# Two kinds of transfer of the rotary attention layers issued by ScalarE instead of SP

## The chip, the core and the metric

The kernel runs on one core of a Trainium2 chip. The metric is the device time of one execution in microseconds, lower is better. In this text TensorE (PE in the profile) does the matrix products, VectorE (DVE) and ScalarE (ACT) work element by element, GpSimd (POOL) adds and fills, and SP is the engine that issues transfers. Each engine takes its own instructions in the order in which they stand; engines wait for each other by semaphores.

## What is computed

```python
x = x + _layernorm(_L0_attn_ref(_layernorm(x), ...))   # one attention block, 16 heads of 8, and an MLP
x = x + _layernorm(_L0_ffn_ref(_layernorm(x), ...))    # L = 4 layers, below

for l in range(L):                       # x is (2, 1024, 128)
    h = _rms(x, ln1_w[l])
    q, k, v = h @ wq, h @ wk, h @ wv     # 16 query heads, 4 key heads, head size 64
    q = q * c + _rot_half(q) * sn        # _rot_half: concatenate([-x[..., 32:], x[..., :32]])
    k = k * c + _rot_half(k) * sn
    attn = softmax(q k^T / 8 + causal_bias)
    x = clip(x + (attn @ v) @ wo, -100, 100)
    x = clip(x + _moe(_rms(x, ln2_w[l]), ...), -100, 100)   # 8 experts, the best 2 weighted
```

All in float32; the kernel splits float32 operands into a high and a low half where precision needs it.

## The kernel before

The first block and its MLP take about the first 600 us. Then come the four layers, each about 675 us: some 500 us in which attention runs, and some 175 us in which the experts run and the next layer's first head is prepared beside them.

Attention is tiled by head group. `n` (0 to 7, `HEADS`) is a pair of a batch row and one of the 4 key heads with its 4 query heads. The 1024 positions of a group are two chunks `c` of 512 columns. For each group and chunk a preparation runs, and its steps have letters that the code uses as names:

- `P`: TensorE projects two query pairs and the key (`u` = 0, 1, 2, three products each), VectorE multiplies each result by the sine table into `rb` and by the cosine table into `ra` (lines 2099 and 2100).
- `R`: four DMAs copy `rb` to `rbp` with the halves of 32 rows swapped (line 1118). They need all three `P` of the chunk, told by the semaphore `s_rp`.
- `A`: GpSimd adds `rbp` to `ra` (line 1240); `H`, `L`, `K`: ScalarE, GpSimd and VectorE split the result into high and low halves; `Q`: five DMAs (lines 1127 and 1131) put them into the stacks `qs`, `ks`.
- `M`: TensorE forms scores of a query tile against keys (line 1756) and VectorE takes row maxima (line 2112). `J`: TensorE turns the maxima (line 1766), ScalarE copies them negated to `mrow` (line 1423), and one DMA writes them into a row of `qs` (line 1138), so that the later product of scores has the maximum subtracted.

Group `n` itself is attended at the same time as group `n + 1` is prepared. A step has a query tile `t` (0 to 7) and a key tile `kt` up to `t`: `S` on TensorE (lines 1784, 1785, and 1787 on the diagonal) into one of two banks, the exponential on ScalarE (line 1416) into one of four `prob` tiles, the running sum on GpSimd (line 1223), `V` on TensorE (line 1801). At the end of a tile come `D` (TensorE line 1816, then VectorE lines 2086 and 2088, the normalised result `att`) and `O` (TensorE line 1823, VectorE line 2207). `S` of a step needs the exponential of the step two before; the exponential needs `V` and the sum of the step four before.

What the engines do in which order isn't written by hand. `network_order()` lists every step with a cost in ns and what it needs (`stage(engine, name, cost, *after)`), and `planned` fills each engine's list greedily by these costs. So a changed cost or engine of one stage moves others. `("sync", ...)` is SP, `("land", ...)` the time until a transfer has landed. Before, `R` stood on SP at 2500 ns and the DMA of `J` on SP at 560 ns, beside all other transfers:

```python
stage("sync", ("R", l, n, c), 2500, ("vector", ("P", l, n, c, u)), ...)
stage("scalar", ("J", l, n, c), 280, ("tensor", ("J", l, n, c)), ...)
stage("sync", ("J", l, n, c), 560, ("scalar", ("J", l, n, c)))
```

In layer 0 the end of the first MLP still runs beside the first group: `Row Nm` (ScalarE line 1292, eight instructions) scales the last rows, after which GpSimd fills stacks with constants (`Zero 1`, lines 1231 to 1234) before it takes up sums and `A` again.

Of the kernel before, what the change touches and what calls it, by code (L numbers as in the profile page):

```python
# [7 lines left out]
F32 = mybir.dt.float32  # L8
# [6 lines left out]
P = 128  # L15
B, SEQ, D = 2, 1024, 128
TPB = SEQ // P
# [8 lines left out]
L, NH, NKV, HD, FF, E = 4, 16, 4, 64, 256, 8  # L26
# [7 lines left out]
NCH = SEQ // CH  # L34
TPC = TPB // NCH
HEADS = NKV * B
# [132 lines left out]
PASSES = NG1 * B  # L169
# [222 lines left out]
def network_order():  # L392
# [72 lines left out]
    def ring_item(l, item):  # L465
# [9 lines left out]
        if what == "P":  # L475
            c, u = part
# [15 lines left out]
            stage("sync", ("R", l, n, c), 2500, ("vector", ("P", l, n, c, u)), older and ("gpsimd", ("A", *older, 2)), *routed)  # L492
            stage("land", ("R", l, n, c), 3400, ("sync", ("R", l, n, c)))
# [3 lines left out]
        elif what == "M":  # L497
            t, m = part
            _, w, k0, k1 = max_pieces(t)[m]
            stage("tensor", ("M", l, n, t, m), w * max(115, (k1 - k0) / 2.2) + (90 + w * 35) * (k1 == (t + 1) * P), ("land", ("Q", l, n, t // TPC)),  # L500
                  ("vector", ("K", l, n, t // TPC)), *turn)
            stage("vector", ("M", l, n, t, m), 150 + 1.04 * w * (k1 - k0), ("tensor", ("M", l, n, t, m)),
                  ("tensor", ("J", l, n - 1, t // TPC)) if n else None)
        else:
            c = part[0]
            if c:
                stage("vector", ("X", l, n), 180, last["vector", "M"])
            stage("tensor", ("J", l, n, c), 200, ("vector", ("X", l, n)) if c else last["vector", "M"], *turn)
            stage("scalar", ("J", l, n, c), 280, ("tensor", ("J", l, n, c)), ("land", ("J", l, n - 1, c)) if n else None)
            stage("sync", ("J", l, n, c), 560, ("scalar", ("J", l, n, c)))  # L510
            stage("land", ("J", l, n, c), 1800, ("sync", ("J", l, n, c)))
# [126 lines left out]
    for b in range(B):  # L638
# [4 lines left out]
             "W", "K", "H", "R", "Q", "J", "A", "X", "L", "D", "O", "V", "S", "P", "M", "Zk", "Za", "Zb", "Zs", "Zv", "Zd", "Zi", "Zr", "Zo"]  # L643
# [10 lines left out]
def program(nc, x_in, ln1_g, ln1_b, Wq, Wk, Wv, Whq, Whk, Wo, ln2_g, ln2_b, W1, b1, W2, b2,  # L654
            f_ln1, f_ln2, wq, wk, wv, wo, wr, wg, wu, wd, cos_in, sin_in, out):
    with ExitStack() as ctx:
# [273 lines left out]
        def _(sp):  # L930
# [115 lines left out]
            for what, *i in NETWORK["sync"]:  # L1046
# [59 lines left out]
                else:  # L1106
                    l, n, c, *part = i
                    b, u = n % 2, (l * HEADS + n) * NCH + c
                    if what == "R":
                        if l and n == 0 and c == 0:  # L1110
                            sp.wait_ge(s_rv, N_ROUTE * B * l)
                            sp.wait_ge(s_gd, 16 * B * l)
                        if u == 0:
                            sp.wait_ge(s_pv1, PASSES * 2 * TPB)
                        sp.wait_ge(s_rp, 6 * u + 6)
                        for k in range(4):
                            to, of = k * 32, (k ^ 1) * 32
                            sp.dma_start(rbp[to:to + 32, :, :], rb[of:of + 32, :, :]).then_inc(s_rot, 16)
                    elif what == "Q" and part[0] == 0:
# [12 lines left out]
                    elif what == "J":  # L1132
                        sp.wait_ge(s_mc, u + 1)
                        if l == 0 and n < 2:
                            sp.wait_ge(s_zero, 3 * n + 3)
                        if l and n == 1:
                            sp.wait_ge(s_qz, NCH * (l - 1) + c + 1)
                        sp.dma_start(qs2[b][0:1, c, :, :].bitcast(F32).rearrange("a h (t n) -> a (h t) n", t=TPC),
                                     mrow2[c][:, :].bitcast(F32)).then_inc(s_rw[c], 16)
# [121 lines left out]
        def _(a):  # L1261
# [100 lines left out]
            for what, *i in NETWORK["scalar"]:  # L1362
# [61 lines left out]
                elif what == "H":  # L1424
# [15 lines left out]
                    else:  # L1440
                        act(ks[b][0:HD, 0, cs], ra[0:HD, 2, :], ACT.Copy).then_inc(s_hi, 1)
                        act(ks[b][HD:P, 1, cs], ra[HD:P, 2, :], ACT.Copy).then_inc(s_hi, 1)
                elif what == "Ge":
# [872 lines left out]
```

## Time and profile before

| what | value |
|---|---|
| median of 3 runs | 3379.39 us (3378.13 to 3379.53) |
| the profiled execution | 3370.07 us, span of its instructions 3368.3 us |
| TensorE busy | 3164.6 us, 94% of the span |
| VectorE, GpSimd, ScalarE busy | 76%, 60%, 51% |
| mean granted clock of TensorE | 0.98 of full speed |

The profiled execution is one execution; its own time is 9.3 us under the median of the runs, and 1.8 us of it lie around the span. Each row of a timeline gives a start in us, a length, the engine and line, what is written and read, the number of merged instructions, and in brackets the time that the engine sat idle before and what ended that. Of the SP queue a row is an issue, that is the time in which the issuing engine is held by it, and not the transfer. A TensorE row ends by a model, so its starts are the better measure. The digits of 40 slices give each engine's busy share in tenths.

### The profile page before, as it was taken

Reading aid. Unit: us, or ns where it says so; the run is one execution under the profiler, and the core shown is the slowest. Engines: PE = TensorE matmul, PEld = TensorE weight load, DVE = VectorE, ACT = ScalarE, POOL = GpSimd, SP = SyncE. Lnnn points to the kernel's source line nnn. Section 1 sums busy time; section 2 is a strip of 40 time slices with the busy share of each in tenths; the row PEclk is TensorE's granted clock in tenths of the full one; section 3 lists DMA queues with packets and bytes.
Section 4 is the critical chain, followed back from the end, with each engine's and each line's share of the span. In section 5 each row is a group of like instructions: output and inputs, shape, how many; then the busy total and the mean of one; then the engine's idle time right before and its main releaser. Section 6 shows DMA issues by size and latency. Waiting matters only on the chain.

```text
span 3368.3 us, 51429 instructions
## 1 busy us (share of the span) xinstructions
PE 3164.6 (94%) x17792; PEld 2094.8 (62%) x17792; DVE 2567.0 (76%) x3764; ACT 1705.9 (51%) x3083; POOL 2010.1 (60%) x1573
## 2 busy tenths in 40 slices
PE   5899998799999999999999999999999999999998
PEld 3455554566666677666666776666667766666576
DVE  7778775777887678778886788778867788788667
ACT  4566667444434474444344755443446553443465
POOL 2100000288868665778777657787776577877765
PEclk8899999899999999999999999999999999999999
DMA  5342421332222154332231543232215532232153
GB/s 121 72 72 51 90 47 37 83 85 67 68 66 69 41 171 136 86 73 64 67 71 31 183 139 86 61 76 67 61 34 187 138 90 60 67 76 60 27 176 114
DMA packets 160402, 283.61 MB, mean 84 GB/s; under 512 B 32592, under 2 KB 64208, under 8 KB 159888
## 3 DMA queue, kind: packets, MB, share of 16 engines
q1 hardware_dynamic: 160144, 280.31, 33.1%
q8 instruction: 145, 2.38, 0.3%
q14 instruction: 113, 0.93, 0.1%
HBM read 88.47 MB, written 31.72 MB: 36 GB/s over the span
## 4 chain that ended last, share of the span: by engine, by line
PE 52%; DVE 6%; ACT 3%; issue 2%; POOL 1%; DMA 1%; SPq 0%; DVEq 0%; ACTq 0%
PE psA L1801 11%; PE psA L1784 7%; PE psA L1756 6%; PE psA L1785 5%; PE psA L1828 3%; PE psA L1829 3%; PE psA L1830 3%; PE psA L1816 3%; DVE rden L2086 2%; PE psA L1823 2%; DVE mxp L2112 2%; PE psA L1865 1%; PE psA L1759 1%; PE psA L1866 1%; PE psA L1867 1%
## 5 line engine op out<-in xcount | busy, mean ns | idle before, releaser
L1416 ACT ACTIVATE prob<-psA 128x512 f32<-128x512 f32 x1152 | 652.7, 595 | 1045.9 <-PE psA L1785 462.3
L1223 POOL TENSOR_TENSOR xw<-xw,prob 128x512 f32<-128x512 f32 x672 | 868.1, 1292 | 230.8 <-ACT prob L1416 157.1
L2112 DVE TENSOR_REDUCE mxp<-psA 128x1 f32<-128x512 f32 (+3 forms) x864 | 528.9, 665 | 57.4 <-PE psA L1756 35.0
L2086 DVE RECIPROCAL rden<-psA 128x256 f32<-128x256 f32 x256 | 449.1, 1754 | 131.3 <-PE psA L1816 128.6
L1784 PE MATMUL psA<-qs,ks 128*128 128x512 f32 x1152 | 523.8, 455 | 21.1 <-ACT prob L1416 19.8
L1756 PE MATMUL psA<-ks,qs 128*128 128x512 f32 (+3 forms) x1536 | 475.4, 385 | 11.3 <-DMA qs<-qs 5.4
L1257 POOL TENSOR_TENSOR hidl<-gate,hidh 128x512 fp32r<-128x512 f32 x256 | 331.3, 1302 | 210.9 <-ACT hidh L1471 209.0
L1785 PE MATMUL psA<-qs,ks 128*128 128x512 f32 x1152 | 453.8, 394 | 0.0
L1223 POOL TENSOR_TENSOR xw<-prob 128x512 f32<-128x512 f32 x224 | 288.1, 1286 | 271.4 <-issue 127.2
L2034 DVE TENSOR_REDUCE mxp<-psA 128x1 f32<-128x1024 f32 x256 | 304.5, 1220 | 84.8 <-PE psA L1591 83.7
L1335 ACT ACTIVATE pr<-psA 128x512 f32<-128x512 f32 x512 | 274.6, 600 | 122.0 <-PE psA L1610 115.8
L1756 PEld LDWEIGHTS psA<-ks,qs 128*128 128x128 f32 x1536 | 269.8, 193 | 84.1 <-issue 32.0
L1784 PEld LDWEIGHTS psA<-qs,ks 128*128 128x128 f32 x1152 | 220.3, 191 | 142.7 <-issue 68.5
L1801 PE MATMUL psA<-prob,vv 128*64 128x256 f32 x2304 | 292.2, 387 | 6.4 <-DVE inner L2207 3.7
L1801 PE MATMUL psA<-prob,outer 128*64 128x256 f32 x2304 | 293.5, 386 | 5.0 <-DVE inner L2207 5.0
L2112 DVE TENSOR_REDUCE mxq<-psA 128x1 f32<-128x384 f32 (+3 forms) x352 | 209.7, 637 | 107.7 <-PE psA L1759 105.6
L1240 POOL TENSOR_TENSOR rab<-rab,rbp 128x512 f32<-128x512 f32 x192 | 247.0, 1301 | 34.9 <-DMA rbp<-rab 34.9
L2238 DVE TENSOR_TENSOR gate<-psA,spread 128x512 f32<-128x512 f32 x256 | 176.1, 688 | 100.5 <-ACT psA L1465 99.0
L1169 POOL TENSOR_TENSOR feat<-feat,smr 128x1024 f32<-128x1024 f32 x16 | 30.6, 1914 | 364.5 <-DVE smr L2017 364.5
L1785 PEld LDWEIGHTS psA<-qs,ks 128*128 128x128 f32 x1152 | 218.4, 190 | 21.5
L1828 PE MATMUL psA<-xh,eh 128*128 128x512 f32 x512 | 210.9, 412 | 17.6 <-DVE gate L2238 10.4
L1801 PEld LDWEIGHTS psA<-prob,vv 128*64 128x64 f32 x2304 | 154.8, 137 | 103.8 <-issue 25.2
(222 smaller groups left out, 5833.0 us busy)
## 6 DMA issues: line engine op xcount, KB each, us to landing
qs<-normed SPq DMA_DIRECT2D x256, 256.0 KB, 4.3
rbp<-rab SPq DMA_DIRECT2D x256, 192.0 KB, 3.5
spread<-routing_weights SPq DMA_DIRECT2D x128, 256.0 KB, 3.6
qs<-qs SPq DMA_DIRECT2D x64, 256.0 KB, 3.2
expert_weight_halves<-eh SPq DMA_DIRECT2D x32, 384.0 KB, 2.4
expert_weight_halves<-el SPq DMA_DIRECT2D x32, 384.0 KB, 3.8
eh<-expert_weight_halves SPq DMA_DIRECT2D x32, 384.0 KB, 3.2
el<-expert_weight_halves SPq DMA_DIRECT2D x32, 384.0 KB, 3.9
```

The lines of the kernel that those rows point to most:

```text
L1223: g.tensor_tensor(psum_k[:, t % 2, :], before, prob[:, i % 4, :], ALU.add).then_inc(s_su, 1 if kt > 1 else 2 + (t == 1))
L1257: g.tensor_tensor(hidl[:, n % 3, :], gate[:, n % GATES, :], hidh[:, n % 3, :], ALU.subtract).then_inc(s_hl, 1)
L1335: act(pr1[:, j % 2, h, :], psS1[:, n % 3, :], ACT.Exp).then_inc(s_ex1, 1)
L1416: act(prob[:, k % 4, :], psS[:, k % 2, :], ACT.Exp, scale=float(HD) ** -0.5).then_inc(s_ex, 1)
L1756: ins = mm(bank[:, i, :], qs1[b][:, c, h + i, t % TPC * P:(t % TPC + 1) * P], ks[b][:, 0, k0:k1], start=(i == 0), stop=not diagonal)
L1784: mm(psS[:, i % 2, :], ks[b][:, 0, tile], qs1[b][:, c, :, qs], start=True, stop=False)
L1785: ins = mm(psS[:, i % 2, :], ks[b][:, 1, tile], qs2[b][:, c, :, qs], start=False, stop=(kt < t))
L1801: ins = mm(psO[t % 2][q * HD:(q + 1) * HD, 0:256], vv[b][:, kt, g * HD:(g + 1) * HD], prob[:, i % 4, q * 256:(q + 1) * 256], start=(kt == ...
L1828: mm(dst, eh[held(w)][:, w0:w0 + P], xh[:, cs], start=True, stop=False)
L2034: vec.tensor_reduce(mxp1[:, p % 2, c, h * 4 + t:h * 4 + t + 1], pair("M", p, c, t, h), AX.X, ALU.max).then_inc(s_mx1, 1)
L2086: vec.reciprocal(rden[:, :], psO[t % 2][:, 256:512]).then_inc(s_rd, 1)
L2112: vec.tensor_reduce(dst, bank, AX.X, ALU.max).then_inc(s_mr, 1)
```

## The change

`R` and the DMA of `J` are issued by ScalarE's own queue. The waits that stood before them on SP go with them to ScalarE. For the planner `R` is a stage of ScalarE of 1200 ns, the DMA of `J` a new stage `Jr` of ScalarE of 300 ns that follows the copy. The transfers themselves, their sizes and the buffers are the same. All else stays on SP.

```diff
-            stage("sync", ("R", l, n, c), 2500, ("vector", ("P", l, n, c, u)), older and ("gpsimd", ("A", *older, 2)), *routed)
-            stage("land", ("R", l, n, c), 3400, ("sync", ("R", l, n, c)))
+            stage("scalar", ("R", l, n, c), 1200, ("vector", ("P", l, n, c, u)), older and ("gpsimd", ("A", *older, 2)), *routed)
+            stage("land", ("R", l, n, c), 3400, ("scalar", ("R", l, n, c)))
...
-            stage("sync", ("J", l, n, c), 560, ("scalar", ("J", l, n, c)))
-            stage("land", ("J", l, n, c), 1800, ("sync", ("J", l, n, c)))
+            stage("scalar", ("Jr", l, n, c), 300, ("scalar", ("J", l, n, c)), ("gpsimd", ("Zero", n)) if l == 0 and n < 2 else None)
+            stage("land", ("J", l, n, c), 2200, ("scalar", ("Jr", l, n, c)))
...
+                elif what == "R":
+                    l, n, c = i
+                    u = (l * HEADS + n) * NCH + c
+                    if l and n == 0 and c == 0:
+                        a.wait_ge(s_rv, N_ROUTE * B * l)
+                        a.wait_ge(s_gd, 16 * B * l)
+                    if u == 0:
+                        a.wait_ge(s_pv1, PASSES * 2 * TPB)
+                    a.wait_ge(s_rp, 6 * u + 6)
+                    for k in range(4):
+                        to, of = k * 32, (k ^ 1) * 32
+                        nc.scalar.dma_start(rbp[to:to + 32, :, :], rb[of:of + 32, :, :]).then_inc(s_rot, 16)
+                elif what == "Jr":
+                    l, n, c = i
+                    u = (l * HEADS + n) * NCH + c
+                    a.wait_ge(s_mc, u + 1)
...
+                    nc.scalar.dma_start(qs2[n % 2][0:1, c, :, :].bitcast(F32).rearrange("a h (t n) -> a (h t) n", t=TPC),
+                                        mrow2[c][:, :].bitcast(F32)).then_inc(s_rw[c], 16)
```

The branches `R` and `J` of SP's list are gone. What ScalarE does in a row, in layer 1 while group 3 is attended and group 4 prepared (`prob<-psA` is an exponential, `mrow` the copy of `J`, `normed<-rab` a step `H`). Before:

```order
617 L1416 ACTIVATE prob<-psA 128x512 x5
618 L1423 ACTIVATE mrow_1<-psA 16x128
619 L1416 ACTIVATE prob<-psA 128x512 x9
620 L1439 ACTIVATE normed<-rab 128x512
621 L1416 ACTIVATE prob<-psA 128x512 x2
```

And now:

```order
675 L1398 ACTIVATE prob<-psA 128x512 x7
676 L1405 ACTIVATE mrow_1<-psA 16x128
677 L1445 DMA qs_1<-mrow_1 1x16x128
678 L1398 ACTIVATE prob<-psA 128x512 x3
679 L1436 DMA rbp<-rab 32x1536 x4
680 L1398 ACTIVATE prob<-psA 128x512 x4
681 L1421 ACTIVATE normed<-rab 128x512
```

The four swaps of chunk 1 stand between the exponentials of the tiles `t = 4`, `kt = 1` and `kt = 2`. TensorE at the same place, the scores of `kt = 2` to `kt = 4` of that tile (lines 1784, 1785) and the product `O` of tile 3 (`wos,att`). Before:

```order
3590 L1784 MATMUL psA<-qs_1,ks 128x512
3591 L1785 MATMUL psA<-qs_1,ks 128x512
3592 L1756 MATMUL psA<-ks,qs_0 128x384
3593 L1759 MATMUL psA<-maskq,identb 128x128
3594 L1784 MATMUL psA<-qs_1,ks 128x512
3595 L1785 MATMUL psA<-qs_1,ks 128x512
3596 L1787 MATMUL psA<-maskk,identb 128x512
3597 L1784 MATMUL psA<-qs_1,ks 128x512
3598 L1785 MATMUL psA<-qs_1,ks 128x512
3599 L1823 MATMUL psA<-wos,att 128x128 x2
```

And now:

```order
3570 L1788 MATMUL psA<-qs_1,ks 128x512
3571 L1789 MATMUL psA<-qs_1,ks 128x512
3572 L1760 MATMUL psA<-ks,qs_0 128x384
3573 L1763 MATMUL psA<-maskq,identb 128x128
3574 L1827 MATMUL psA<-wos,att 128x128 x2
3575 L1788 MATMUL psA<-qs_1,ks 128x512
3576 L1789 MATMUL psA<-qs_1,ks 128x512
3577 L1791 MATMUL psA<-maskk,identb 128x512
```

`O` of tile 3 has moved ahead of two products of scores. ScalarE at the start of layer 0, where group 1 is prepared; `inner<-qT,rstd` is `Row Nm`. Before:

```order
219 L1285 ACT_TABLE_LOAD
220 L1285 ACTIVATE std<-vsum,eps 128x8
221 L1292 ACTIVATE inner<-qT,rstd 128x128 x8
222 L1423 ACTIVATE mrow_1<-psA 16x128
223 L1377 ACTIVATE normed<-inner 128x512 x2
```

And now:

```order
223 L1267 ACT_TABLE_LOAD
224 L1267 ACTIVATE std<-vsum,eps 128x8
225 L1405 ACTIVATE mrow_1<-psA 16x128
226 L1445 DMA qs_0<-mrow_1 1x16x128
227 L1436 DMA rbp<-rab 32x1536 x4
228 L1274 ACTIVATE inner<-qT,rstd 128x128 x8
```

`Row Nm` now stands behind the copy of maxima and behind five issues.

## Rows read from the trace of the kernel before

**Rows 1.** The page: busy us of each engine, share of the span, instructions.

```profile
PE 3164.6 (94%) x17792; PEld 2094.8 (62%) x17792; DVE 2567.0 (76%) x3764; ACT 1705.9 (51%) x3083; POOL 2010.1 (60%) x1573
```

**Rows 2.** TensorE: who it waited for; us in total, times, longest us.

```profile
PE psA L1823 <- DVE att L2088: 31.2, 35, 1.1
...
PE psA L1784 <- ACT prob L1416: 19.8, 43, 2.3
...
PE psA L1756 <- DMA qs<-qs: 5.4, 3, 2.4
```

**Rows 3.** SP's queue: what it waited for, same columns.

```profile
SPq L1138 <- ACT mrow L1423: 519.9, 60, 36.4
SPq L1118 <- DVE rab L2100: 335.1, 59, 10.0
```

**Rows 4.** SP's issues by line: count, ns min/median/max, first and last start.

```profile
L1118 SPq DMA_DIRECT2D rbp<-rab x256: 507/591/1786, 606.0 to 3110.2; - x128
...
L1138 SPq DMA_DIRECT2D qs<-mrow x64: 526/563/575, 639.9 to 3164.6; - x64
...
L1127 SPq DMA_DIRECT2D qs<-normed x256: 598/660/2005, 614.7 to 3122.8; - x128
...
L1105 SPq DMA_DIRECT2D spread<-routing_weights x128: 319/327/1253, 1145.9 to 3334.6; - x128
```

**Rows 5.** Windows: length; busy us (count) of PE, PEld, DVE, ACT, POOL; clock; DMA.

```profile
600.00:700.00 100.00, 82.76 (x392) 53.86 (x392) 71.97 (x120) 46.63 (x89) 43.44 (x34) 0.86 0.37 94
...
1498.90:1562.15 63.25, 61.64 (x379) 40.57 (x379) 50.41 (x78) 25.41 (x46) 48.36 (x39) 1.00 0.29 68
```

**Rows 6.** Timeline, ScalarE: start, us, line, tiles, count, idle time before.

```profile
1556.49 0.60 ACT L1416 ACTIVATE prob<-psA 128x512 f32<-128x512 f32 x1 [0.88 <-PE psA L1787]
1560.44 1.09 ACT L1416 ACTIVATE prob<-psA 128x512 f32<-128x512 f32 x2 [3.35 <-PE psA L1785]
1562.18 1.08 ACT L1416 ACTIVATE prob<-psA 128x512 f32<-128x512 f32 x2 [0.65 <-PE psA L1785]
```

**Rows 7.** Timeline, SP's queue: start, us, line, count.

```profile
1560.63 2.46 SPq L1118 DMA_DIRECT2D rbp<-rab  x4
```

**Rows 8.** Timeline, VectorE.

```profile
1559.92 0.68 DVE L2100 TENSOR_TENSOR rab<-psA,cosT 128x512 f32<-128x512 f32 x1
...
1562.30 0.42 DVE L2088 TENSOR_TENSOR att<-psA,rden 128x256 f32<-128x256 f32 x1
```

**Rows 9.** Timeline, TensorE.

```profile
1562.83 0.50 PE L1784 MATMUL psA<-qs,ks 128*128 128x512 f32 x1
...
1564.09 0.61 PE L1823 MATMUL psA<-wos,att 128*128 128x128 f32 x4
1564.45 0.42 PE L1756 MATMUL psA<-ks,qs 128*128 128x384 f32 x1
```

**Rows 10.** Timeline, TensorE, three waits around a group.

```profile
1547.05 0.71 PE L1823 MATMUL psA<-wos,att 128*128 128x128 f32 x4 [0.96 <-DVE att L2088]
...
1548.53 0.83 PE L1801 MATMUL psA<-prob,outer 128*64 128x256 f32 x5 [0.31 <-DVE inner L2207]
...
1586.52 0.50 PE L1784 MATMUL psA<-qs,ks 128*128 128x512 f32 x1 [0.29 <-ACT prob L1416]
```

**Rows 11.** Timeline, VectorE, between two chunks.

```profile
1589.26 5.47 DVE L2112 TENSOR_REDUCE mxp<-psA 128x1 f32<-128x512 f32 x9 [1.03 <-PE psA L1756]
```

**Rows 12.** Timeline, ScalarE and GpSimd, start of layer 0.

```profile
667.88 2.44 ACT L1292 ACTIVATE inner<-qT,rstd 128x128 f32<-128x128 f32 x8 [4.72 <-DVE rstd L1979]
670.26 0.27 ACT L1423 ACTIVATE mrow<-psA 16x128 fp32r<-16x128 f32 x1
...
670.38 3.50 POOL L1231 MEMSET qs<- 64x4096 f32 x1 [21.75 <-ACT inner L1292]
...
675.91 1.26 POOL L1223 TENSOR_TENSOR xw<-prob 128x512 f32<-128x512 f32 x1
```

**Rows 13.** Timeline, GpSimd, a change from experts to attention.

```profile
1272.68 3.80 POOL L1240 TENSOR_TENSOR rab<-rab,rbp 128x512 f32<-128x512 f32 x3 [1.81 <-DMA rbp<-rab]
```

More of the change, by code:

```diff
@@ L642, in network_order @@
              "Ew", "Eh", "El", "Es", "Er", "Hf", "Hw", "Hh", "Hl", "Si", "Y", "Ug", "Uu", "Aw", "Wa", "Wb",
-             "W", "K", "H", "R", "Q", "J", "A", "X", "L", "D", "O", "V", "S", "P", "M", "Zk", "Za", "Zb", "Zs", "Zv", "Zd", "Zi", "Zr", "Zo"]
+             "W", "K", "H", "R", "Q", "J", "Jr", "A", "X", "L", "D", "O", "V", "S", "P", "M", "Zk", "Za", "Zb", "Zs", "Zv", "Zd", "Zi", "Zr", "Zo"]
     return planned(plan, kinds, 150, 150, "VD", 110, {"vector": 120})
@@ L1108, in _ @@
                     b, u = n % 2, (l * HEADS + n) * NCH + c
[L1109 to L1119, printed above, removed]
+                    if what == "Q" and part[0] == 0:
                         if l and n == 1:
@@ L1131, in _ @@
                         sp.dma_start(qs2[b][HD:P, c, 0:GQ:2, :].bitcast(F32), qs2[b][0:HD, c, 1:GQ:2, :].bitcast(F32)).then_inc(s_dup, 16)
[L1132 to L1139, printed above, removed]
             sp.wait_ge(s_out, 16 * NCH * B)
@@ L1442, in _ @@
                         act(ks[b][HD:P, 1, cs], ra[HD:P, 2, :], ACT.Copy).then_inc(s_hi, 1)
+                elif what == "R":
[14 more added lines that the diff above has]
+                    a.wait_ge(s_mc, u + 1)
+                    if l == 0 and n < 2:
+                        a.wait_ge(s_zero, 3 * n + 3)
+                    if l and n == 1:
+                        a.wait_ge(s_qz, NCH * (l - 1) + c + 1)
+                    nc.scalar.dma_start(qs2[n % 2][0:1, c, :, :].bitcast(F32).rearrange("a h (t n) -> a (h t) n", t=TPC),
+                                        mrow2[c][:, :].bitcast(F32)).then_inc(s_rw[c], 16)
                 elif what == "Ge":
```

## The prediction

> **What bounds the kernel now.** I read the page first. TensorE is busy for 3164.6 us of 3368.3, the other engines for 76% or less [rows 1], so there are about 204 us in all in which TensorE is not at work, and nothing that merely relieves SP can give back more. Then the windows. While a group is attended the pattern repeats exactly every 63.25 us, with TensorE busy for 61.6 of it at full clock and ScalarE for 25.4 [rows 5]. The first 100 us of the layers are looser: TensorE 82.8 of 100 [rows 5]. Then who waits. TensorE's waits for transfers of the layers come to 5.4 us in three places, and its longest named waits in the layers are 31.2 us for `att` of VectorE and 19.8 us for exponentials [rows 2]. SP waits 519.9 us at the row of maxima and 335.1 us at the swap [rows 3]: it stands there before its data exist, it isn't late with them. In the group shown the swaps are issued at 1560.63 [rows 7], 0.03 us after the multiplication that they need has ended, at 1559.92 + 0.68 = 1560.60 [rows 8]. So the queue that the change relieves delays nearly nothing, and the engine that it loads sits in a loop (scores, exponential, values) with TensorE.
>
> **What moves.** 256 swaps of 0.591 us and 64 rows of 0.563 us [rows 4] are 151 + 36 = 187 us of issuing that leave SP and go to ScalarE. ScalarE's busy time doesn't show an issue, but the engine can't start an exponential during it. Per chunk that is four issues, 2.46 us [rows 7], and one of 0.56 us. No row shows an issue from ScalarE. The nearest are SP's own of the same transfers, 0.59 us each. From below the shortest plain issue bounds it, 0.327 us, from above that of the other transfers between buffers on the chip, 0.660 us at the median, 0.83 us in a row of four (3.32 us) [rows 4]. I take SP's 0.59.
>
> Perfetto Trace Analysis in the Trainium skill (section DMA Instruction, HWDGE) says that the recorded window of an issue is the time in which the issuing sequencer is held, lock and descriptors included, and Advanced Engine Details and Errata (Clock Domains) gives SP's and ScalarE's sequencers the same clock. By these the 0.59 us would hold on ScalarE as well, and the sum would be mine; the rows of before show issues on SP alone.
>
> **The row of maxima (`Jr`).** It follows the copy on ScalarE, which was the releaser on SP as well. In the loop ScalarE sat idle 0.88 us after the copy of chunk 1 before the next exponential, which waited for TensorE [rows 6]; 0.56 us fits in. In chunk 0 the planner's new order puts the copy ahead of an exponential that waits for `V` anyway. I cost `Jr` at nothing; without that cover it would be 64 x 0.56 = 36 us at most.
>
> **The swap of chunk 1.** By the new order it stands between the exponentials of `kt = 1` and `kt = 2` of tile 4. The first two exponentials start at 1560.44 and, 0.49 us later, at 1560.93, and end at 1561.53; that of `kt = 2` starts at 1562.18 [rows 6]. The sine products are ready at 1560.60. The issues can begin when the second exponential has started, 1560.93, or at the latest when it has ended, 1561.53. They end at 1563.39 or 1563.99, and the exponential is ready 0.60 us after that: 1563.99 or 1564.59. TensorE needs it for the scores of `kt = 4`, at 1562.83 before [rows 9]. Now `O` of tile 3 stands ahead of these, 1564.45 - 1564.09 = 0.36 us [rows 9], with its `att` ready at 1562.72 [rows 8]; TensorE gets to the scores at 1563.19. The stall is 0.80 to 1.40 us. I take 0.85, near the lower end, since two exponentials in a row take 1.09 us and not 1.20 [rows 6]: ScalarE takes its next instruction while the last runs. There are 24 such places (groups 2 to 7 of 4 layers): + 20.4 us (19 to 34).
>
> **The swap of chunk 0.** It stands behind the exponential of `kt = 1` of tile 7. Between the scores whose exponential it delays and those that need that exponential, the new order has another product of scores, five maxima pieces, a block of values and a `D`, over 2.5 us of TensorE's work by TensorE's pace [rows 9], 0.2 to 0.5 us each,. The cost is between nothing and chunk 1's 0.85 us; I take nothing. Without the cover it would be 20 x 0.85 = 17 us.
>
> **The new order.** Around a group TensorE waits three times, 0.96 + 0.31 + 0.29 = 1.56 us [rows 10]. The first two come from VectorE, late with `D` and `O` because it ran through its maxima late: it sat idle for 1.03 us before their first [rows 11], while TensorE did three blocks of values. The new list puts the first maxima pieces directly behind the scores, moves `O` and `D` of VectorE, and puts the fifth block of values ahead of the sixth scores, so that the 0.29 us go. Against that the `D` that TensorE waits for has one maxima piece more ahead of it, about 0.6 us (5.47 us for 9) [rows 11]. Bounds are 0 and 1.56 us per group. I take a third, 0.5 us, in 20 places (groups 3 to 7): - 10 us (0 to - 31).
>
> **Layer 0.** Here the window had TensorE idle for 17 us [rows 5]. Before, `Row Nm` ran from 667.88 to 670.32, and only then could GpSimd fill the stacks, 670.38 to 675.8, before it took up sums at 675.91 [rows 12] and worked on without a pause. Now the copy of maxima (not before 670.26), its issue and the four swaps come first: 670.26 + 0.27 + 0.56 + 2.46 = 673.6, and `Row Nm` ends 2.44 us later, at 676.0. GpSimd starts 5.7 us late. Sums and `A` queue behind it, and TensorE's `D` and ScalarE's exponentials behind these. TensorE idles there, so a part is covered: + 4 us (0 to 5.7).
>
> **The three changes from experts to attention.** The swap of the next layer's first chunk stands between steps of expert units. GpSimd's two next steps are then about 2.5 us later and end some 1.1 us after the 1272.68 at which it took up the rotation, having idled 1.81 us before it [rows 13]. The rotation's transfers then end TensorE's wait of up to 2.4 us for `qs` [rows 2]. With 0.4 us for the second chunk, 1.5 us each: + 4.5 us (0 to 10).
>
> **The sum.** 20.4 - 10 + 4 + 4.5 = + 18.9 us. Against the profiled execution's own 3370.07 us that is 3389.0. The median of the runs is 9.3 us above that execution; I carry this difference over unchanged: 3379.4 + 18.9 = 3398 us. A change under 0.2%, 6.8 us, I count as none: a measurement of this kernel can't tell it.
>
> DMA: Bandwidth & Descriptors in the Trainium skill (section Issuing engines are not separate DMA queues) says that issuing from several engines saves the issuing sequencer's time alone, as the transfers run on the same DMA engines. The trace agrees as far as it goes: what is saved is time of a queue that waits 519.9 and 335.1 us for its data [rows 3]. By that rule alone the time would stay 3379; the rule counts no loss where the other queue belongs to an engine with work.
>
> **Rivals.**
> 1. Faster: VectorE catches up wholly. Its 1.03 us go and with them all 1.56 us of TensorE's waits per group, - 31 us. This decides once more than 1.45 us per group come back, since the rest costs 28.9; with 0.59 us per issue it ends at 3377. With an issue of 0.45 us the stall of chunk 1 is 0.85 - 0.55 = 0.3 us, 7 us in all, the rest about 6, and the time 3362. For it: VectorE's idle time is real, and TensorE's work per group is the same. Against it: the extra maxima piece.
> 2. Issues on ScalarE at 0.33 us: 1.3 us for four, ending at 1562.2, no stall. Then - 10 + 2.5 + 2.5 = - 5: 3374. For it nothing in the trace but that plain issues are that short [rows 4]; the swaps never were under 0.507.
> 3. Issues at 0.83 us: 3.32 us for four, a stall of 1.71 us in 24 places, 41 us, with 5 and 6 for the rest and 10 back: 3421. This would also come from both queues contending for one generator of descriptors; in the attention of a group SP has nothing to issue at these moments, which speaks against it.
> 4. The stall is there but is covered: the 0.85 us come back at the later waits of the same group, as these wait for VectorE and not for TensorE. Then 8.5 + 3 us at most are left less 10: 3381. Against it: between the stall and the next wait VectorE waits for TensorE, so a shift of TensorE shifts both.
>
> **Chances.** The forecast with its own range, 3386 to 3410, has 0.47, of which 0.02 lie within 0.2%. Rival 1 has 0.14, half of it under 3372.6; rival 2 0.15, a third of it under that; rival 3 0.10; rival 4 0.14, of which 0.03 lie under and 0.01 over. That gives faster 0.15 (0.07 + 0.05 + 0.03), within 0.2% 0.29 (0.02 + 0.07 + 0.10 + 0.10), slower 0.56 (0.45 + 0.10 + 0.01). The range from 3367 to 3418 leaves the far half of rival 1 and most of rival 3 out.
>
> **What the profile after would show.** Issues in ScalarE's queue, 256 and 64, with their length: 0.59 right, 0.33 or 0.83 the rivals. A second queue of transfers in the list of DMA queues, at the same bytes. In a group a TensorE wait of about 0.9 us for `prob` at the scores of the diagonal of tile 4, and waits for `att` that are shorter than 0.96. The period of a group at 63.6 us instead of 63.25; 62.0 or less would be rival 1, 64.3 rival 3. GpSimd's first fill at 676 instead of 670.4. SP's waits at the two lines gone, and nobody served earlier for it. Wrong would be the prediction if ScalarE ran its queue's issues beside its own exponentials, or if the planner's order of VectorE decided alone.

## The result, and the profile after

The changed kernel takes 3426.52 us (median of 4 runs, 3425.76 to 3430.72) where the kernel before took 3379.46: a ratio of 1.0144, 95% interval 1.0129 to 1.0159, 47 us slower. The forecast was slower, 3398, and the time lies outside its range. The profiled execution of the changed kernel took 3430.72 us, 4.2 over its median; that of before was 9.4 under its own. The two traces therefore differ by 60.6 us and not by 47.

The page after, with the lines that answer to [rows 1]: busy times; queues of transfers (packets, MB, share of 16 engines); the chain that ended last, by line.

```profile
PE 3193.7 (93%) x17792; PEld 2101.0 (61%) x17792; DVE 2583.4 (75%) x3764; ACT 1701.4 (50%) x3083; POOL 2004.8 (58%) x1573
...
q1 hardware_dynamic: 145808, 229.43, 26.4%
q10 hardware_dynamic: 14336, 50.88, 6.3%
...
PE psA L1805 11%; PE psA L1788 6%; PE psA L1760 6%; PE psA L1789 5%; PE psA L1832 3%; PE psA L1833 3%; PE psA L1834 3%; PE psA L1820 2%; ACTq L1436 2%; PE psA L1827 2%; DVE rden L2090 2%; PE psA L1869 1%; PE psA L1870 1%; PE psA L1871 1%; PE psA L1791 1%
```

TensorE's busy time grew by 29 us without an added product. Some 12 of them are time at a lower clock (the paragraph on the clock below). A steady group shows 0.66 us more each, which makes another 16 in 24 groups; the ends of products are modelled, so a part of a stall can be counted as busy. A second queue, q10, carries the 50.88 MB of swaps and rows. ScalarE's issues (ACTq) stand in the chain that ended last with 2%. Their lengths (count, ns min/median/max, first and last start), which answer to [rows 4]:

```profile
L1436 ACTq DMA_DIRECT2D rbp<-rab x256: 514/612/1839, 608.9 to 3169.3; - x128
...
L1445 ACTq DMA_DIRECT2D qs<-mrow x64: 516/527/550, 644.0 to 3225.1; - x64
```

0.61 and 0.53 us hold ScalarE as they held SP. The swaps land 3.5 us after their issue, as they did before. TensorE's waits, as in [rows 2]:

```profile
PE psA L1788 <- ACT prob L1398: 51.4, 73, 2.8
...
PE psA L1827 <- DVE att L2092: 21.6, 36, 1.0
...
PE psA L1742 <- ACT vv L1390: 7.6, 4, 2.3
```

The waits for exponentials rose from 19.8 us in 43 places to 51.4 in 73, those for `att` fell from 31.2 to 21.6. Those for `vv`, ScalarE's copies of projected values, rose from 0.9 us in 3 places to 7.6 in 4; the prediction had not looked at them. The window of one steady group, as in [rows 5] (length, busy us of PE, PEld, DVE, ACT, POOL, clock, DMA share, GB/s):

```profile
1562.10:1625.88 63.78, 62.30 (x380) 40.54 (x379) 50.97 (x78) 25.36 (x47) 48.23 (x39) 1.00 0.29 67
```

The period is 63.78 us (63.25 before). In it, at the place of [rows 6, 9], ScalarE and its queue, and then TensorE:

```profile
1651.15 0.60 ACT L1398 ACTIVATE prob<-psA 128x512 f32<-128x512 f32 x1 [3.35 <-PE psA L1789]
1651.63 0.52 ACTq L1436 DMA_DIRECT2D rbp<-rab  x1
1651.65 0.59 ACT L1398 ACTIVATE prob<-psA 128x512 f32<-128x512 f32 x1
1652.18 1.90 ACTq L1436 DMA_DIRECT2D rbp<-rab  x3
1654.21 1.09 ACT L1398 ACTIVATE prob<-psA 128x512 f32<-128x512 f32 x2 [1.97 <-POOL xw L1205]
```

```profile
1654.86 0.50 PE L1788 MATMUL psA<-qs,ks 128*128 128x512 f32 x1 [0.66 <-ACT prob L1398]
```

The first issue starts when the second exponential does, the last ends 2.45 us later, the next exponential starts 0.13 us after it and TensorE's scores 0.65 us after that. The releaser named for that exponential is GpSimd's sum, but the 1.97 us end where the issues end. The start of layer 0, as in [rows 12]:

```profile
670.22 0.27 ACT L1405 ACTIVATE mrow<-psA 16x128 fp32r<-16x128 f32 x1 [4.07 <-PE psA L1770]
670.51 0.52 ACTq L1445 DMA_DIRECT2D qs<-mrow  x1
671.07 2.55 ACTq L1436 DMA_DIRECT2D rbp<-rab  x4
673.66 2.45 ACT L1274 ACTIVATE inner<-qT,rstd 128x128 f32<-128x128 f32 x8 [3.18 <-issue]
...
676.17 3.51 POOL L1213 MEMSET qs<- 64x4096 f32 x1 [25.13 <-ACT inner L1274]
```

The fill came at 676.17, where the prediction had 676.

To see where the time went I took the start of the scores of `kt = 0` for tiles 0 and 4 of each group on TensorE, in both traces, and added up the differences by stretch. "Up to tile 4" of group 1 means from the first scores of the layer to that start. The last three columns are traces of experiments told below: the new order with SP's issues (e1_new_order), the old order with ScalarE's (e2_old_order), and the split order with SP's (e5_split_order).

| stretch | before, us | after | e1 | e2 | e5 |
|---|---|---|---|---|---|
| up to the first scores of the layers | 642.4 | +3.7 | +7.0 | +6.0 | +6.0 |
| layer 0: groups 0 and 1 up to tile 4 | 110.3 | +9.0 | +4.6 | +2.4 | -0.1 |
| layers 1 to 3: the same stretch | 276.5 | +9.0 | -1.8 | +5.1 | 0.0 |
| the three changes of layer, from tile 4 of group 7 | 628.6 | +19.0 | +8.9 | +9.7 | +1.8 |
| groups 2 to 7, 24 steps from tile 4 to tile 4 | 1511.0 | +19.8 | -11.3 | +33.7 | -11.5 |
| the end | 199.5 | +0.2 | -0.1 | +0.3 | -0.1 |
| all | 3368.3 | +60.6 | +7.4 | +57.3 | -4.0 |

The first row is hardly an effect of the change: in all 14 experiments that stretch was 1.5 to 10 us longer than in the one execution of before, also in e5, where every list is that of before up to there (6.0). The mean of the 15 traces is 5.3, and so about half of the 9.4 us by which that execution lay under its median belongs there. The row of the changes has a scatter of its own: in e3, e5 and e6, which keep the order of before there and issue the swaps, or all but two of a chunk's four, from SP, it is 1.7 to 3.2 us.

### The profile page after: what moved, and what is told of

Read it like the earlier page. It is cut to its first block, busy times and chain, and to the rows that moved or that the text cites. A ratio compares the mean times of both kernels' runs of the same rounds, so it can differ in the third digit from the quotient of the medians.

```text
span 3428.9 us, 51429 instructions
## 1 busy us (share of the span) xinstructions
PE 3193.7 (93%) x17792; PEld 2101.0 (61%) x17792; DVE 2583.4 (75%) x3764; ACT 1701.4 (50%) x3083; POOL 2004.8 (58%) x1573
## 3 DMA queue, kind: packets, MB, share of 16 engines
q10 hardware_dynamic: 14336, 50.88, 6.3%
## 4 chain that ended last, share of the span: by engine, by line
PE 50%; DVE 6%; ACT 3%; issue 2%; ACTq 2%; POOL 1%; DMA 1%; DVEq 0%; POOLq 0%
PE psA L1805 11%; PE psA L1788 6%; PE psA L1760 6%; PE psA L1789 5%; PE psA L1832 3%; PE psA L1833 3%; PE psA L1834 3%; PE psA L1820 2%; ACTq L1436 2%; PE psA L1827 2%; DVE rden L2090 2%; PE psA L1869 1%; PE psA L1870 1%; PE psA L1871 1%; PE psA L1791 1%
## 5 line engine op out<-in xcount | busy, mean ns | idle before, releaser
L1398 ACT ACTIVATE prob<-psA 128x512 f32<-128x512 f32 x1152 | 645.4, 595 | 996.9 <-PE psA L1789 335.6
L1788 PE MATMUL psA<-qs,ks 128*128 128x512 f32 x1152 | 537.0, 466 | 51.7 <-ACT prob L1398 51.4
L2116 DVE TENSOR_REDUCE mxp<-psA 128x1 f32<-128x512 f32 (+3 forms) x864 | 535.9, 664 | 63.7 <-PE psA L1763 34.9
L1789 PE MATMUL psA<-qs,ks 128*128 128x512 f32 x1152 | 457.5, 397 | 0.0
L1222 POOL TENSOR_TENSOR rab<-rab,rbp 128x512 f32<-128x512 f32 x192 | 246.5, 1289 | 40.5 <-DMA rbp<-rab 40.5
```

The source lines that it names most:

```text
L1398: act(prob[:, k % 4, :], psS[:, k % 2, :], ACT.Exp, scale=float(HD) ** -0.5).then_inc(s_ex, 1)
L1788: mm(psS[:, i % 2, :], ks[b][:, 0, tile], qs1[b][:, c, :, qs], start=True, stop=False)
L1789: ins = mm(psS[:, i % 2, :], ks[b][:, 1, tile], qs2[b][:, c, :, qs], start=False, stop=(kt < t))
L2116: vec.tensor_reduce(dst, bank, AX.X, ALU.max).then_inc(s_mr, 1)
```

## The experiments

Each kernel is made from the changed one by a function that says how many of the four swaps of a chunk, and whether the row, ScalarE issues. What it doesn't issue goes into SP's list, at the place that the planner's own sequence of steps gives it; all other lists stay. In the traces the arithmetic of TensorE, VectorE, GpSimd and ScalarE stands exactly in the order of before in e2, e3, e4, e6, e7 and e10, and exactly in that of after in e1, e8, e13 and e14; only the issues differ. The cut shown is that of e4 (`4 * c`, `False`).

```diff
+def by_scalar(what, l, n, c):
+    return (4 * c) if what == "R" else (False)
...
+                        for k in range(by_scalar(what, l, n, c), 4):
+                            to, of = k * 32, (k ^ 1) * 32
+                            sp.dma_start(rbp[to:to + 32, :, :], rb[of:of + 32, :, :]).then_inc(s_rot, 16)
...
-                    for k in range(4):
+                    for k in range(by_scalar(what, l, n, c)):
                         to, of = k * 32, (k ^ 1) * 32
                         nc.scalar.dma_start(rbp[to:to + 32, :, :], rb[of:of + 32, :, :]).then_inc(s_rot, 16)
```

In the table `r` is the first value (how many of the four swaps ScalarE issues), `jr` the second (whether it issues the row), `n` the prepared group, `c` its chunk, and the ratio is that to the kernel before in the same series. The kernel before had medians of 3375.4, 3375.4, 3375.4 and 3377.1 us in the four series of experiments, and 3379.5 in that of the result, so kernels of different series are compared by their ratios.

| run | planner's costs | r | jr | median us | ratio (95%) |
|---|---|---|---|---|---|
| e1_new_order | after | 0 | no | 3380.9 | 1.0015 (1.0005 to 1.0025) |
| e2_old_order | before | 4 | yes | 3426.9 | 1.0150 (1.0133 to 1.0168) |
| e3_rows_only | before | 0 | yes | 3375.6 | 0.9995 (0.9986 to 1.0005) |
| e4_chunk1 | before | 4 * c | no | 3413.0 | 1.0107 (1.0091 to 1.0123) |
| e10_chunk0 | before | 4 * (1 - c) | no | 3388.7 | 1.0037 (1.0024 to 1.0050) |
| e6_two_of_four | before | 2 * c | no | 3378.3 | 1.0004 (0.9995 to 1.0013) |
| e7_later_place | before | 4 * c, later | no | 3398.1 | 1.0060 (1.0046 to 1.0075) |
| e9_true_cost | R 2450, Jr 560 | 4 | yes | 3431.5 | 1.0168 (1.0153 to 1.0183) |
| e5_split_order | after for n > 1 | 0 | no | 3364.5 | 0.9963 (0.9949 to 0.9976) |
| e12_split_scalar | after for n > 1 | 4 | yes | 3412.6 | 1.0109 (1.0094 to 1.0124) |
| e11_rows_first | after, Nm moved | 4 | yes | 3428.9 | 1.0159 (1.0142 to 1.0176) |
| e8_first_by_sp | after | 4 * (n > 0) | yes | 3425.5 | 1.0146 (1.0132 to 1.0160) |
| e13_groups_only | after | 4 * (n > 1) | yes | 3424.4 | 1.0135 (1.0119 to 1.0151) |
| e14_changes_only | after | 4 * (n < 2) | yes | 3395.9 | 1.0052 (1.0039 to 1.0065) |

**Order or queue: e1_new_order and e2_old_order.**

> TensorE, VectorE, GpSimd and ScalarE do their work in the order of the changed kernel, but swaps and rows are issued by SP as before, each at the place in SP's list where the planner put it. Theory A, the queue costs all: the time is that of before, 3379 us or a few less, and by the prediction's own term for the new order 3369. Theory B, the new order itself costs TensorE its pace (in the group's trace TensorE's idle time is 0.1 us shorter than before and yet the period 0.5 us longer): the period stays near 63.7 us and the time between 3395 and 3415. In the trace the stall of 0.66 us for prob in tile 4 should be gone by both.

> The order of the kernel before on all engines, with the four swaps and the row issued by ScalarE at the places that they had in time in the old plan. Theory A: 3379 plus the stalls of ScalarE; by the prediction's terms 20.4 + 4 + 4.5 = 3408, or the full 3427 if the queue costs all. Theory B: 3395 to 3405, and together with the new order's own excess it makes the 47 us. A stall of 0.8 to 1.4 us per group for prob should stand in tile 4 behind the swap of chunk 1.

The queue costs nearly all of it: old order with ScalarE's issues 1.0150, new order with SP's 1.0015. Theory B falls. It rose from TensorE's idle time in the steady group, 1.48 us after against 1.61 before, and that figure misleads, as a stall is partly counted as busy. The window of a steady group of e1, and the waits of e1 and then of e2:

```profile
1544.63:1607.26 62.63, 61.81 (x380) 40.48 (x379) 50.79 (x79) 25.47 (x47) 48.35 (x39) 1.00 0.29 68
```

```profile
PE psA L1868 <- DVE att L2133: 24.1, 35, 1.1
PE psA L1829 <- ACT prob L1439: 17.2, 35, 2.8
```

```profile
PE psA L1829 <- ACT prob L1439: 51.3, 71, 1.6
PE psA L1868 <- DVE att L2133: 31.1, 35, 1.1
```

With SP's issues the new order is 0.62 us per group shorter than before; TensorE's idle time in it is 62.63 - 61.81 = 0.82 us, against 63.25 - 61.64 = 1.61. The kernel as a whole gains nothing from it, since the new order loses as much elsewhere (the table of stretches).

**Rows and chunks: e3_rows_only, e4_chunk1, e10_chunk0.**

> The order of the kernel before; only the DMA of the row of maxima is issued by ScalarE, the swaps by SP. The prediction costs it at nothing, 3379, with 36 us (3415) as its bound without cover. A rival that every issue on ScalarE costs its 0.56 us once per chunk would give 3415.

> The order of the kernel before; only the swaps of the second chunk of each group are issued by ScalarE, all else by SP. By the prediction 24 stalls of 0.85 us, 3379 + 20 = 3400 (bounds 19 and 34). If the stall is covered by the later waits of the same group, 3381 to 3385.

> The order of before; only the swaps of chunk 0 are issued by ScalarE, all else by SP: the counterpart of the run with chunk 1 alone. By the prediction and by the trace with both they cost nothing in the groups and 2.5 us at each of the three changes of layer, where P of chunk 1 comes that much later: 3375.5 + 8 = 3383. If they cost 0.61 us per issue wherever they stand, 3375 + 70 = 3440 at most; if neither, 3375.

Rows cost nothing that can be measured, in the old order. The swaps of chunk 1 cost 1.07%, 36 us, above the 20 expected and over the upper bound of 34. The 0.85 us behind the 20 had counted 0.36 us of `O` ahead of the scores, which stands there in the new order alone; the expectation for the old order should have had 1.2 us a place. Those of chunk 0 cost 0.37%; its trace shows 0.1 us in each of the groups 2 to 7 and 3.1 us at each change of layer, 12.5 us with layer 0, and the median came out 6 us above the 3383. The three ratios add up to 1.4%, that of e2 is 1.5%. ScalarE's queue, ScalarE and TensorE in e4 at the stall:

```profile
1645.59 1.90 ACTq L1477 DMA_DIRECT2D rbp<-rab  x3
1647.61 1.09 ACT L1439 ACTIVATE prob<-psA 128x512 f32<-128x512 f32 x2 [1.96 <-POOL xw L1246]
...
1648.26 0.50 PE L1829 MATMUL psA<-qs,ks 128*128 128x512 f32 x1 [1.28 <-ACT prob L1439]
```

TensorE stands idle for 1.28 us there, once per group.

**How the stall grows: e6_two_of_four and e7_later_place.**

> The order of before; of the four swaps of chunk 1 two are issued by ScalarE, at the same place as with all four, and two by SP; all else by SP. If ScalarE is simply held for the length of each issue (0.61 us), two fewer take 1.23 off the stall of 1.33 us per group: 0.1 us is left, the time 3380 to 3383. If the stall is a fixed cost of issuing there at all, or of the transfers coming over two queues, it stays at about 1.3 us per group and the time at 3413. Half of it would be 3397.

> The order of before; all four swaps of chunk 1 by ScalarE, but in groups 2 to 7 they stand two exponentials later, behind that of kt = 3 of tile 4, where ScalarE idled 2.36 us. If only the place costs, ScalarE's stall goes to 0.1 us per group; GpSimd's rotation then comes 1.2 to 2.5 us later, which is covered or costs up to 1.2 us a group: 3384 to 3389 if covered (8 us stay at the places of group 1 and the changes of layer), up to 3410 if not. If issues on ScalarE cost wherever they stand, 3413.

```diff
+    for l in range(L):
+        for n in range(2, HEADS):
+            new["scalar"].remove(("R", l, n, 1))
+            new["scalar"].insert(new["scalar"].index(("S", l, n - 1, 4, 3)) + 1, ("R", l, n, 1))
```

With two issues the stall is 0.09 us per group and the time that of before. Two issues end early enough for the exponential (e6, ScalarE's queue and ScalarE):

```profile
1632.13 0.67 ACTq L1477 DMA_DIRECT2D rbp<-rab  x1
1632.93 1.09 ACT L1439 ACTIVATE prob<-psA 128x512 f32<-128x512 f32 x2 [0.73 <-PE psA L1830]
```

Two issues fewer are 1.23 us less, and the stall, by the starts of the scores behind it, is 0.09 where it was 1.31. So the price is the length of the issues beyond the slack (the time that ScalarE has to spare there); it is neither fixed nor does it come from the use of two queues. Two exponentials later (e7) the stall for the scores of tile 4 is gone, but 0.69 us per group stay. GpSimd, ScalarE, TensorE:

```profile
1649.49 2.54 POOL L1267 TENSOR_TENSOR rab<-rab,rbp 128x512 f32<-128x512 f32 x2 [0.62 <-DMA rbp<-rab]
...
1653.39 0.60 ACT L1443 ACTIVATE prob<-psA 128x512 f32<-128x512 f32 x1 [1.24 <-POOL xw L1250]
...
1654.13 0.47 PE L1833 MATMUL psA<-qs,ks 128*128 128x512 f32 x1 [0.73 <-ACT prob L1443]
```

The rotation on GpSimd waits for transfers that were issued 2.0 us later than SP issued them in the kernel before, a running sum waits behind it, and the exponential waits for the sum. At either place something is due.

**The planner's cost: e9_true_cost.**

> The changed kernel, but the planner is told what the traces show the issues to hold ScalarE for: 2450 ns for the four swaps instead of 1200, 560 ns for the row instead of 300. In the steady groups it then puts the swap of chunk 1 ahead of the first exponential of tile 4 instead of behind the second. If the planner's halved cost is at fault, the stall of 1.2 us per group goes and the time falls from 3426 to 3395 or less. If an issue block of 2.46 us has no free place at that point, since the sine products are ready only when the exponentials are due, the exponentials behind it wait as long or longer: 3420 to 3445.

Told the true length, the planner makes the steady group longer, not shorter (window of a group):

```profile
1562.85:1628.03 65.18, 61.93 (x381) 40.59 (x380) 50.44 (x78) 25.12 (x46) 49.35 (x39) 1.00 0.29 66
```

65.18 us, of them 3.25 idle on TensorE; so the halved costs weren't the fault. From tile 4 to tile 4 the groups of this run take 64.6 to 67.2 us. Those of 65.6 and more are the nine in which TensorE's clock went down, as in the group after the one shown (TensorE, two of three stalls, then a window of 1 us behind them):

```profile
1639.06 0.71 PE L1868 MATMUL psA<-wos,att 128*128 128x128 f32 x4 [1.21 <-DVE att L2133]
1640.35 0.47 PE L1772 MATMUL psA<-xh,wah 128*128 128x512 f32 x1 [0.57 <-DVE mxp L2157]
```

```profile
1642.00:1643.00 1.00, 1.00 (x8) 0.64 (x6) 1.00 (x2) 0.60 (x1) 0.09 (x1) 0.50 0.00 0
```

The mean granted clock of this kernel's runs is 0.974, where it is 0.980 in those of before. By an estimate (0.006 of 3430) that makes about 20 of the 56 us that it is slower than before.

**The new order's places: e5_split_order and e12_split_scalar.**

> All issues by SP. The planner sees the changed kernel's costs only for groups 2 to 7 of each layer, so that every engine keeps the order of before up to the start of group 1 (t = 4 in it) and in the change to the next layer, and has the changed kernel's order in the steady groups. If the new order is worth 0.56 us in each of 20 steady groups (11.3 us in the trace with the new order and SP's issues) and its losses (5.1 us at the start of layer 0, 8.9 at the changes of layer) belong to the places kept as before, 3379 - 11 = 3368, or 3363 to 3373 if the 5.0 us of the step inside group 1 are lost or not. If the gain is only borrowed from those places, 3376 to 3381.

> The split order (that of the changed kernel in the steady groups, that of before elsewhere) with all swaps and rows issued by ScalarE. If order and queue add up: 3364.5 for the split order, plus 1.2 us in 24 groups and 1.3 in four, 34 us, plus 8 at the changes of layer and 3 to 5 in layer 0 and the first groups = 3409 to 3412. If they don't add, because the new order's slack is what the issues eat, 3420 or more.

```diff
+            as_new = n > 1
+            stage("scalar" if as_new else "sync", ("R", l, n, c), 1200 if as_new else 2500, ("vector", ("P", l, n, c, u)), older and ("gpsimd", ("A", *older, 2)), *routed)
```

(The same for the row and for the landings.) The gain of the steady groups stays, 11.5 us in the trace and 11 us in the medians, and the losses go: 3364.5 us is less than either kernel. Here SP issues everything; it is the planner's new order that pays. With ScalarE's issues the same order gives 3412.6, just over the 3409 to 3412 that the sum gave: order and queue add up.

**Layer 0 and the changes of layer: e11_rows_first, e8_first_by_sp, e13_groups_only, e14_changes_only.**

> The changed kernel, but on ScalarE the two last steps Row Nm of layer 0 stand, as before, ahead of the copy of maxima, its row and the swaps. If their late place is what costs the start of layer 0 its 8.3 us, GpSimd's first fill comes 5 us earlier and the step from tile 4 of group 0 to group 1 loses about 5 us: 3421. If the issues or the rest of the new order there cost it, it stays at 3426.

```diff
+    early = new["scalar"].index(("J", 0, 0, 1))
+    for c in (3, 2):
+        new["scalar"].remove(("Row", "Nm", 4, c))
+        new["scalar"].insert(early, ("Row", "Nm", 4, c))
```

> The changed kernel in its own order, but the swaps of each layer's first group (n = 0) are issued by SP; those of groups 1 to 7 and the rows by ScalarE. By the traces the three changes of layer lose 10 us to the queue, of which P of chunk 1 being 2.1 to 2.4 us late behind the swap of chunk 0 is 6 to 7 us: the time goes from 3426 to 3416 to 3421. If the transfers of weights make these changes long and not the queue, it stays at 3426.

> The changed kernel in its own order; the swaps of groups 0 and 1 of each layer are issued by SP, those of groups 2 to 7 and all rows by ScalarE. If the loss at the changes of layer is real, it goes: about 1.3 us in each of 24 groups remain over the same order with SP's issues, 3381 + 31 = 3412. If it belongs to the one profiled execution, the time stays above 3420.

> The reverse: the changed kernel in its own order, with the swaps of groups 0 and 1 and all rows issued by ScalarE, those of groups 2 to 7 by SP. If the loss at the changes of layer is real, 3381 + 15 to 25 = 3396 to 3406, with three or four more stretches of TensorE at half clock than the same order with SP's issues has. If not, 3381 to 3388.

With `Row Nm` ahead, the start of layer 0 is 2.7 us shorter in the trace and the median no less: that place is not what costs most there. With group 0's swaps on SP (e8) the changes of layer are 7.8 us shorter in the trace, and the median 1 us, which 4 runs can't tell from nothing; the 3416 to 3421 expected did not come. e13 and e14 settle more. By the ratios the swaps of groups 2 to 7 alone cost 1.20% over e1, 40.5 us, nearly everything, and those of groups 0 and 1 alone 0.37%, 12.5 us; together, in the changed kernel, they cost 1.29%, 43.6 us. The parts add up to 9 us more than the whole, at the edge of what the intervals can tell; it suggests that the places at the changes partly cover one another. e13 missed its 3412. In its trace the steady groups cost the 31 us expected over e1, and 12.5 more are lost between the first scores of the layers 1 to 3 and tile 4 of group 1. The swap of chunk 0 of group 2 is issued there, while group 0 is attended, where there is no cover. In the changed kernel, layer 1, ScalarE's queue, ScalarE, TensorE:

```profile
1417.82 3.30 ACTq L1436 DMA_DIRECT2D rbp<-rab  x4
1421.25 1.09 ACT L1398 ACTIVATE prob<-psA 128x512 f32<-128x512 f32 x2 [3.97 <-issue]
...
1421.90 0.50 PE L1788 MATMUL psA<-qs,ks 128*128 128x512 f32 x1 [1.85 <-ACT prob L1398]
```

After this stall of 1.85 us TensorE's clock goes down. The same stretch by windows of 1 us, the last three columns being granted clock, DMA share and GB/s (0.50 is 1.2 GHz, 1.00 is 2.4):

```profile
1421.00:1422.00 1.00, 0.10 (x1) 0.11 (x1) 0.71 (x2) 0.75 (x2) 0.08 (x1) 1.00 0.89 203
...
1423.00:1424.00 1.00, 1.00 (x6) 0.88 (x4) 0.59 (x1) 0.57 (x2) 0.82 (x2) 0.50 0.01 0
1424.00:1425.00 1.00, 1.00 (x4) 0.89 (x4) 0.11 (x1) 0.28 (x1) 0.86 (x2) 0.50 0.00 0
...
1426.00:1427.00 1.00, 1.00 (x7) 0.88 (x7) 0.28 (x1) 0.00 (x0) 1.00 (x2) 0.89 0.00 0
```

And at the change of layer before it, where the prediction had looked at GpSimd, it is the copies `vv` that stand behind the swap of chunk 0:

```profile
1284.48 2.49 ACTq L1436 DMA_DIRECT2D rbp<-rab  x4
1287.06 1.09 ACT L1390 ACTIVATE vv<-psA 128x512 f32<-128x512 f32 x2 [2.62 <-issue]
...
1287.81 0.36 PE L1742 MATMUL psA<-wvh,xh 128*128 128x256 f32 x1 [1.65 <-ACT vv L1390]
```

## Why the prediction was right or wrong

**Right.** What bounds the kernel, and that a relieved SP serves nobody earlier: in e3 the rows leave SP and in e6 two of the four swaps of chunk 1, and neither kernel is faster (0.9995 and 1.0004). The length of an issue on ScalarE, 0.61 us where 0.59 was taken, which removes rivals 2 and 3. `Jr` at nothing (e3, in the old order). The mechanism and the place of the stall of chunk 1: the row at 1654.86, whose 0.66 us are less than the stall, since the product before it ends by a model. The shorter waits for `att`. The new order's gain in the groups: 10 us forecast, 11.3 measured; the direction had a reason, the third of 1.56 us that was taken had none, so the size was partly luck. The fill of layer 0 at 676. Rival 1 was wrong: VectorE's idle time went in part only (0.62 us of the 1.56 a group came back in e1). Rival 4 too: between e1 and after, the stall's delay of TensorE's scores is 0.91 us behind tile 4 and still there, undiminished, at the end of each group.

**The stall of chunk 1, mis-sized.** Taken at 0.85 us from the bounds 0.80 to 1.40. Against e1, which has the same order, it is 0.9 to 0.93 by the starts of the scores. What was missing is the 0.13 us between the end of the last issue and the next exponential.

**The swap of chunk 0, costed at nothing.** In the old order this is right in the steady groups (e2 against e4, 0.05 us a group). In the new order it adds 0.24 us in the group shown. The exponential behind it started 0.13 us after the last issue, whatever releaser is named:

```profile
1679.42 2.44 ACTq L1436 DMA_DIRECT2D rbp<-rab  x4
1681.99 1.08 ACT L1398 ACTIVATE prob<-psA 128x512 f32<-128x512 f32 x2 [3.08 <-POOL xw L1205]
```

Both together are 1.17 us in that group, and over all 24 the queue costs 19.8 + 11.3 = 31 us instead of 20.4. The cover had been read off the changed order of TensorE with the timing of before; 2.44 us of issues in 2.5 us of work leave no margin.

**The changes of layer and the first groups, the step that failed.** The term was + 4.5 us for the three changes, with a bound of 10. The swaps that are issued in the first groups of layers 1 to 3, those of group 1 and chunk 0 of group 2, had no term at all. In the trace this part is + 28.0 (9.0 + 19.0). About 7 of it are the new order itself, which the prediction had costed in the steady groups and at the start of layer 0 alone; in e5, which keeps the old order there, they are gone (1.8). 21 are the queue. At the changes the delay was followed on one engine, GpSimd, while the swap also held up the copies `vv` (7.6 us in four waits of TensorE, 0.6 in e1). In group 0 it held up exponentials for which TensorE had no other work in reserve (1.85 us at the place shown).

How much this is in the medians can be estimated. The steady groups take + 19.1 to + 20.0 us in all five traces with this order there and ScalarE's issues for groups 2 to 7 (after, e8, e11, e12, e13), so their 19.8 may be taken as fixed. Of the 47 us of the medians some 27 then lie outside the steady groups, where the forecast had 8.5; in the steady groups it had 10.4.

**Layer 0**: + 4 forecast, + 9.0 in the trace, of which 4.6 are the order (e1) and the rest the issues. The late `Row Nm`, which was the whole argument, is worth at most 2.7 by the trace of e11.

**The clock, not thought of.** TensorE's busy time from 640 us on at the lower clock, of which half is lost, costs some 19 us in the trace before, 15 in e1 and 31 after. The steady groups of these three have none of it; most of what after has more stands behind stalls in the first groups. In the medians the part is smaller: the mean granted clock of the runs is 0.978 after and 0.9795 in e1 and before, which is 5 us by an estimate. e8 has the changed kernel's order, 21 us in its trace, and the same median. The windows from tile 4 of group 0 to group 1 in layer 1, after and then e1, with the same 281 products:

```profile
1381.07:1434.08 53.01, 47.99 (x281) 32.85 (x281) 36.79 (x53) 27.78 (x53) 42.48 (x35) 0.94 0.38 87
```

```profile
1370.79:1419.38 48.59, 44.70 (x281) 30.81 (x281) 36.35 (x53) 27.17 (x53) 41.17 (x34) 1.00 0.41 94
```

Of the 4.4 us between them 3.3 are TensorE's longer busy time, at the lower clock (0.94 on average), and 1.1 are stalls.

By terms, in the trace: 20.4 became 31.0, -10 became -11.3, 4 became 9.0, 4.5 became 28.0, which is 18.9 against 56.7, with 3.9 us outside the layers. In the medians the sum is 47. The 13.6 us that the traces have beyond it come from the two executions that happened to be profiled. How they divide among the terms stays open. e8 and e13 suggest that some lie in the changes of layer: these are 8 us shorter in their traces than in that of after, and the medians differ by 1 to 3 us. Open too is why the new order loses 1.7 us between tiles 0 and 4 of group 1 in each of the layers 1 to 3, and what in it costs the changes of layer their 8.9 us in e1.

## What to carry to other kernels

An issue costs the engine that makes it its full length, and the kernel what exceeds the slack at that very place: two of them were free where four cost 1.3 us per group. Moving issues to an engine inside the loop that sets the pace can pay only if somebody waited for the old queue; here the waits of that queue were waits for data. When a planner moves other work along with the edit, run the new order with the old queue and the old order with the new queue: here the two halves had opposite signs in the steady groups (+ 31 us for the queue, - 11.3 for the order, in the traces), and the useful one, kept in the places where it helps, made a kernel 0.37% faster than before.

## What the runs showed of the hardware

The first issue began at 1651.63, while the exponential ahead of it in the list ran from 1651.65 to 1652.24: an issue doesn't wait for the end of the arithmetic before it. The arithmetic behind it does wait: the next exponential started 0.13 us after the last issue's end.

A stall of TensorE of 1.85 us was followed, 0.9 us after it took up work, by about 3.4 us at a granted clock of 0.50, that is 1.2 GHz, and so cost about as much again. The single stall of 0.7 to 1.3 us in each group of after, e2 and e4 was not followed by it. But neither the length of a stall nor its being alone decides. In e9 three stalls of 0.59, 1.21 and up to 0.58 us, 2.4 and 1.3 us apart, stand in 20 groups; in 9 of them the clock fell at the second stall or within 2.4 us behind it, in 11 it did not. And in e1 a stall of 2.33 us was not, with full clock for the whole window around it; the kernel before has the same stall, and there the clock fell:

```profile
1220.03 0.47 PE L1873 MATMUL psA<-xh,eh 128*128 128x512 f32 x1 [2.33 <-DVE gate L2283]
```

```profile
1216.00:1230.00 14.00, 9.19 (x43) 6.58 (x42) 13.35 (x28) 8.52 (x14) 5.29 (x4) 1.00 0.39 124
```

What decides between the two isn't shown by these runs.
